# One attention kernel: values as streamed probabilities or as column-tile weights

## What is computed

```python
x = x + attention(layernorm(x))        # 32 query heads, 8 key/value heads, head size 32, rotary, causal
x = x + fake_quant(layernorm(x)) @ fake_quant(ctx)
x = x + fixed_point_linear(layernorm(x))   # Q8.8 integers, 16 bit results
# attention, per batch and head:
scores = q @ k.T / sqrt(32); scores[causal] = min
ctx = softmax(scores) @ v              # heads h*4 .. h*4+3 share one k and v
```

## Time and profile before

| what | value |
|---|---|
| median of three runs | 586.71 us |
| profiled execution | 589.05 us, span of its instructions 587.2 us |
| TensorE matmul busy | 492.4 us (84%) |
| VectorE, ScalarE, GpSimd busy | 394.1, 327.5, 259.5 us |
| mean granted TensorE clock | 0.952 |
| attention groups | from 146.65 us to about 434.4 us of the span |

### The profile page before, as it was taken

The page is one execution under the profiler, slowest core; times in us unless marked ns, Lnnn a source line. Parts: engine busy times, 40 slices in busy tenths (PEclk is TensorE's granted clock), DMA queues, the critical chain, the costliest instruction groups (busy, mean ns, idle before and its releaser), DMA issues.

```text
span 587.2 us, 12002 instructions
## 1 busy us (share of the span) xinstructions
PE 492.4 (84%) x4050; PEld 279.8 (48%) x4050; DVE 394.1 (67%) x763; ACT 327.5 (56%) x395; POOL 259.5 (44%) x242
## 2 busy tenths in 40 slices
PE   2678998587689889898899999999798999976776
PEld 2356643233355555455565555555443444444333
DVE  5875277464587788787866877887439466767436
ACT  2654233200577766677757888888943531456533
POOL 5030113324367779767784555456652734230000
PEclk9898998779999999999969999999999899987899
DMA  9821366522301110011103222112355110000015
GB/s 313 255 86 59 115 178 173 148 88 89 90 2 47 45 45 18 29 44 45 48 22 133 91 93 90 39 52 91 109 204 220 42 36 19 1 2 1 33 42 215
DMA packets 42616, 50.68 MB, mean 86 GB/s; under 512 B 4049, under 2 KB 32337, under 8 KB 42577
## 3 DMA queue, kind: packets, MB, share of 16 engines
q1 hardware_dynamic: 25792, 41.69, 21.3%
q10 hardware_dynamic: 16784, 8.46, 5.0%
HBM read 40.57 MB, written 9.44 MB: 85 GB/s over the span
## 4 chain that ended last, share of the span: by engine, by line
PE 37%; DVE 19%; DMA 12%; issue 11%; POOL 10%; ACT 7%; SPq 3%; DVEq 0%; ACTq 0%; POOLq 0%
PE ps L1352 10%; DMA rope_scratch<-s1reg 7%; PE ps L1457 4%; PE ps L1220 4%; DVE stat L725 4%; PE ps L1179 3%; PE ps L1414 3%; DMA qstack<-rope_scratch 3%; POOL s1reg L1092 3%; PE ps L1240 2%; PE ps L1207 2%; DVE mt L781 2%; PE ps L1255 2%; POOL wkv L1100 2%; POOL s1reg L1111 2%
## 5 line engine op out<-in xcount | busy, mean ns | idle before, releaser
L781 DVE TENSOR_REDUCE mt<-ps 128x1 f32<-128x512 f32 (+3 forms) x256 | 113.2, 484 | 50.3 <-PE ps L1222 47.9
L1179 PE MATMUL ps<-xT,wqx 128*128 128x512 f16 x384 | 99.3, 397 | 3.9 <-DVE s1reg L772 3.5
L1352 PE MATMUL ps<-wo_reg,xT 128*128 128x512 f16 x384 | 94.2, 384 | 2.3 <-DVE wqx L813 2.2
L1111 POOL TENSOR_TENSOR s1reg<-s1reg 128x1280 f16<-128x1280 f32 x32 | 83.7, 2614 | 28.1 <-ACT s1reg L510 26.5
L503 ACT ACTIVATE s1reg<-ps 128x1280 f32<-128x1280 f32 x64 | 78.9, 1233 | 24.4 <-PE ps L1242 22.5
L1220 PE MATMUL ps<-kreg,qstack 96*128 (+4 forms) x256 | 72.4, 314 | 22.1 <-DVE mt L781 15.3
L510 ACT ACTIVATE s1reg<-s1reg 128x1280 f16<-128x1280 f32 x64 | 81.3, 1270 | 2.8
L1240 PE MATMUL ps<-qstack,kreg 98*128 (+4 forms) x256 | 58.0, 303 | 11.8 <-DMA qstack<-mrow 8.3
L797 DVE TENSOR_TENSOR s1reg<-s1reg 128x1280 f16<-128x1280 f32 x32 | 53.3, 1667 | 15.1 <-ACT s1reg L510 15.1
L1100 POOL TENSOR_TENSOR wkv<-wkv 128x128 f32<-128x128 f32 x64 | 35.1, 549 | 62.4 <-DVE rcp L803 62.3
L1179 PEld LDWEIGHTS ps<-xT,wqx 128*128 128x128 f16 (+1 forms) x384 | 35.6, 102 | 43.7 <-issue 13.8
(11 more groups left out here) (123 smaller groups left out, 790.0 us busy)
## 6 DMA issues: line engine op xcount, KB each, us to landing
s1reg<-in_ctx SPq DMA_DIRECT2D x16, 512.0 KB, 4.6
qstack<-rope_scratch SPq DMA_DIRECT2D x48, 128.0 KB, 2.4
rope_scratch<-s1reg SPq DMA_DIRECT2D x40, 128.0 KB
qstack<-in_x SPq DMA_DIRECT2D x8, 512.0 KB, 5.3
s1reg<-in_L_attn_Wq ACTq DMA_DIRECT2D x8, 512.0 KB, 4.8
s1reg<-in_L_attn_Wo ACTq DMA_DIRECT2D x8, 512.0 KB, 5.3
s1reg<-in_x SPq DMA_DIRECT2D x16, 256.0 KB, 2.9
out<-s1reg SPq DMA_DIRECT2D x7, 512.0 KB, 2.7
```

The source lines that it names most:

```text
L781: nc.vector.reduce_max(mt[:, 2 * hp + e, qt:qt + 1], ps[:, 3 + e, 0:P * (qt + 1)], AX.X).then_inc(s_max, 1)
L1111: nc.gpsimd.tensor_tensor(pl[:, j % 2, :], ebuf[:, j % 2, :], ph[:, j % 2, :], ALU.subtract).then_inc(pl_done[1], 1)
L1179: last = mm(out_ap, w(ws, k), xT[:, xs, KT * b + k, :], start=(k == 0 and n == 0), stop=(k == KT - 1 and n == 2))
L1352: last = mm(ps[:, bank, :], xT[:, os, KT * b + k, t], wo_sb[:, ws, 4 * h:4 * h + 4, k, :], start=(k == 0 and n == 0), stop=(k == KT - 1 an ...
```

## The change

The probabilities become the streamed operand and the values the weights. `values(G)` is one block for four heads. It has five products: for the denominators a 128x32 block of ones as weights, with the high and then the low parts of the probabilities streamed; for the numerators the high values with the high probabilities, the low values with the high, and the high values with the low. Each product has four key blocks k with 512, 384, 256 and 128 columns and for each the four heads, head j writing output partitions 32j to 32j+31: 80 products and 80 weight loads per group. The result is already transposed, in bank NUM (5) and, for the sums, bank DEN (6). `out_transpose`, `pv_out`, `inverse_sum` and `head_out` go. VectorE's `heads_norm` takes the reciprocal of the whole DEN bank (128x512) and multiplies it with NUM into `osum`; it stands where `ot_low` stood, before maxima 6 and 7. `ot_high` reads `osum`, moves behind `p_high(G,2)` on ScalarE, and `ot_low` moves to GpSimd. In phase D `p_low(G,2)` moves from VectorE to GpSimd. Probabilities get six buffers instead of two, so that `p_high` and `p_low` no longer wait for the values of two heads before. `values(G-1)` stands in group G behind `scores_t(G,1)`. All loops are written out as 16 groups.

```diff
-VW = 2 * DH + 1
+VW = 2 * DH
+SLOTS = 6
...
-        def attention_c(eng, body):
-            body(0, 0, False, True)
-            with eng.Fori(1, KV - 1) as g:
-                body(g, g, True, True)
-            body(KV - 1, KV - 1, True, True)
-
-        def attention_d(eng, body):
-            body(KV, 0, True, True, 0, 0)
-            body(KV + 1, 1, True, True, 0, 1)
-            with eng.Fori(1, KV // 2 - 1) as p:
-                for u in range(2):
-                    body(p * 2 + (KV + u), p * 2 + u, True, True, p, u)
-            body(NG - 2, KV - 2, True, True, KV // 2 - 1, 0)
-            body(NG - 1, KV - 1, True, False, KV // 2 - 1, 1)
+        def attention_c(body):
+            for g in range(KV):
+                body(g, g, g > 0, True)
+
+        def attention_d(body):
+            for g in range(KV):
+                body(KV + g, g, True, g < KV - 1, g // 2, g % 2)
...
             def exp(G, j):
                 act.wait_ge(st_done, G * 4 + (j + 1))
-                if not (isinstance(G, int) and G == 0 and j < 2):
-                    act.wait_ge(*pl_count(G, j))
+                if G or j >= 2:
+                    act.wait_ge(pl_done[(j + 2) % HG], G + (j >= 2))
...
             def p_high(G, j):
                 act.wait_ge(e_done, G * 4 + (j + 1))
-                if not (isinstance(G, int) and G == 0 and j < 2):
-                    act.wait_ge(pv_done, G * 4 + (j - 1))
-                nc.scalar.activation(ph[:, j % 2, :], ebuf[:, j % 2, :], ACT.Copy).then_inc(ph_done, 1)
+                p_free(act, HG * G + j)
+                nc.scalar.activation(ph(HG * G + j), ebuf[:, j % 2, :], ACT.Copy).then_inc(ph_done, 1)
...
             def ot_high(G):
-                act.wait_ge(ot_done, G + 1)
-                nc.scalar.activation(xT[:, 0, one(G), :], ps[:, OT:OT + 1, :], ACT.Copy).then_inc(ot_hi, 1)
+                act.wait_ge(o_norm, G + 1)
+                nc.scalar.activation(xT[:, 0, G, :], osum, ACT.Copy).then_inc(ot_hi, 1)
...
                 p_high(G, 1)
-                pv_out(G, 0)
+                exp(G, 2)
+                p_high(G, 2)
                 if tail:
                     ot_high(G - 1)
-                exp(G, 2)
-                p_high(G, 2)
                 if ahead:
                     max_row(G + 1)
-                pv_out(G, 1)
...
+            def heads_norm(G):
+                dve.wait_ge(den_done, G + 1)
+                nc.vector.reciprocal(rsum[:, :], ps[:, DEN, :]).then_inc(o_rcp, 1)
+                dve.wait_ge(pv_done, G + 1)
+                dve.wait_ge(o_rcp, G + 1)
+                if G:
+                    dve.wait_ge(ot_lo, G)
+                nc.vector.tensor_tensor(osum, ps[:, NUM, :], rsum[:, :], ALU.mult).then_inc(o_norm, 1)
...
                 ahead_max(5)
                 middle()
                 if tail:
-                    ot_low(G - 1)
+                    heads_norm(G - 1)
                 ahead_max(6, 7)
                 if ahead:
                     split_max(G + 1)
-                p_low(G, 2)
-                inverse_sum(G, 1)
+                if G < KV:
+                    p_low(G, 2)
...
+            def ot_low(G):
+                pool.wait_ge(ot_hi, G + 1)
+                nc.gpsimd.tensor_tensor(xT[:, 1, G, :], osum, xT[:, 0, G, :], ALU.subtract).then_inc(ot_lo, 1)
 
             def body(G, g, tail, ahead, p=None, u=None):
+                p_low(G, 1)
+                if p is not None:
+                    p_low(G, 2)
                 if tail:
-                    head_out(G - 1, 3)
-                p_low(G, 1)
-                head_out(G, 0)
-                head_out(G, 1)
+                    ot_low(G - 1)
                 p_low(G, 3)
-                head_out(G, 2)
...
-            def values(G, j):
-
-                low, before = pl_count(G, j)
-                pe.wait_ge(low, before + 1)
-                if not (isinstance(G, int) and G == 0 and j == 0):
-                    pe.wait_ge(pvs_done, G * 4 + j)
-                for qt in range(TT):
-                    for k in range(qt + 1):
-                        at = SEG[k] + P * (qt - k)
-                        for n, part in enumerate((ph, pl)):
-                            last = mm(ps[:, PV, VW * qt:VW * qt + VW], part[:, j % 2, at:at + P],
-                                      vext[:, k, one(G), :], start=(k == 0 and n == 0), stop=(k == qt and n == 1))
-                last.then_inc(pv_done, 1)
...
+            def values(G):
+
+                for j in range(HG):
+                    pe.wait_ge(pl_done[j], G + 1)
+                pe.wait_ge(mrow_ready, min(G + 2, NG))
+                if G:
+                    pe.wait_ge(o_norm, G)
+
+                def product(bank, part, weight, first, final):
+                    for k in range(TT):
+                        n = T - P * k
+                        for j in range(HG):
+                            last = mm(ps[DH * j:DH * j + DH, bank, P * k:T], weight(k), part(HG * G + j)[:, SEG[k]:SEG[k] + n],
+                                      start=(first and k == 0), stop=(final and k == TT - 1))
+                    return last
+
+                product(DEN, ph, lambda k: ones_h[:, 0:DH], True, False)
+                product(DEN, pl, lambda k: ones_h[:, 0:DH], False, True).then_inc(den_done, 1)
+                product(NUM, ph, lambda k: vext[:, k, G, 0:DH], True, False)
+                product(NUM, ph, lambda k: vext[:, k, G, DH:2 * DH], False, False)
+                product(NUM, pl, lambda k: vext[:, k, G, 0:DH], False, True).then_inc(pv_done, 1)
...
                 ahead_scores(1)
+                scores_t(G, slot, 1)
                 if tail:
-                    values(G - 1, 3)
-                scores_t(G, slot, 1)
+                    values(G - 1)
                 ahead_scores(2)
...
-                    pe.wait_ge(pvs_done, 4 * NG)
+                    pe.wait_ge(o_norm, NG)
```

More of the change, by code:

```diff
@@ L123, in build, with ph, pl @@
         wkvf = wkv[:, :, :, :, :].rearrange("p s n k c -> p (s n k c)").bitcast(F32)
-        ogrp = wkvf[:, 0:512].rearrange("p (t c) -> p t c", t=TT)
-        osum = wkvf[:, 512:640].rearrange("p (t c) -> p t c", t=TT)
-        pvs = wkvf[:, 640:640 + 2 * TT * VW].rearrange("p (s t c) -> p s t c", s=2, t=TT)
+        osum = wkvf[:, 3072:3584]
+        p_slots = [(s1reg, 2560), (s1reg, 3840), (wkvf, 0), (wkvf, 1792)]
+        ppair = [region[:, at:at + SCORES].bitcast(F16).rearrange("p (s n) -> p s n", s=2) for region, at in p_slots]
+        ppair += [more[:, 2 * SCORES * i:2 * SCORES * i + 2 * SCORES].rearrange("p (s n) -> p s n", s=2) for i in range(2)]
+        def ph(head):
+            return ppair[head % SLOTS][:, 0, :]
+        def pl(head):
+            return ppair[head % SLOTS][:, 1, :]
         ctx_st = s1reg[:, 5120:7168].rearrange("p (s n) -> p s n", s=2)
@@ L1227, in max_transpose @@
                     pe.wait_ge(rope_mul, 12)
-                if not (isinstance(G, int) and G < 2):
-                    pe.wait_ge(ot_lo, G - 1)
+                if G >= 2:
+                    pe.wait_ge(o_rcp, G - 1)
                 nc.tensor.transpose(mt_ps(G), mh[:, :, :].rearrange("p s n -> p (s n)"), ident_h).then_inc(mt_done, 1)
```

116 lines of the change are left out of this document (32 added, 84 removed).

## The result

The changed kernel takes 680.9 us (median of four runs, 678.88 to 681.2) against 586.13 us for the kernel before beside it (583.99 to 589.8): ratio 1.157, 95% interval 1.152 to 1.161. The profiled execution takes 680.65 us with a span of 678.9 us; before it was 589.05 and 587.2. So 91.6 us are to be explained on the profiled executions, where the prediction had 57 or 58. The mean granted TensorE clock is 0.888, before 0.952. TensorE's matmuls are busy 526.3 us (78% of the span), VectorE 437.9, ScalarE 309.4, GpSimd 233.0.

The account below looks back on a forecast made before the run. Bound: nearly full TensorE and a loop through VectorE's maxima. Phase C +18, group 8 +2, phase D +25, last group +4, group 0 -1, loops -3, clock +12: +57 or 58, 589.05 to 647 us (645 against the median); range 611 to 685.

Parts of the forecast that it names:

- The loop through VectorE: Every group: what stands in VectorE's list before maxima 6 and 7 delays the next group; 3.2 us more there.
- The reciprocal: VectorE's 128x512 division in heads_norm: 3.2 us, bounds 0.68 and 4.3.
- slow division: Rival: VectorE's reciprocal takes eight plain passes, 4.3 us, making the kernel 661 us; chance 0.2.
- The values block: TensorE's 80 products per group: four column tiles stream together, taking 3.1 us.
- The layout of a group: Phase D laid out from durations: max_transpose at 17.6 us, next start 21.1, 4.2 more than 16.92; phase C 20.8.
- The clock: TensorE's pause from 12.9 to 17.6 lowers its clock in each group: 0.8 us each, 12 in all, between 0 and 1.7.
- Group 8: Given phase C's period of 20.8 us, against 18.95 before: 2 us more.
- Last group: No scores ahead; values end at 21.9, column_sums at 24.3 us instead of 20.0: 4.3 more.
- Loops: Looped groups cost 0.37 us more than unrolled, 3.7 for ten; 3 us taken off.
- Cheap division: Rival: VectorE's reciprocal runs as any operation there, 0.68 us, giving 600 us; chance 0.07.
- Tiles in turn: Rival: TensorE's column tiles do not overlap, values take 11.0 us per group, about 760 us in all; chance 0.08.
- a kernel bound by TensorE: Rival: VectorE's stretch between maxima 5 and 6 stays under 0.7 us, groups take 16.0, kernel 559 us; chance 0.03.

Follow-up runs that it names:

- short_division: Changed kernel with the reciprocal run on only 4 of the 512 columns of the denominator bank: 600.12 us, ratio 1.016.
- scalar_division: Changed kernel with narrower low-part waits in groups 8 and 9 and the reciprocal on ScalarE as exp(-ln x): 591.98 us, ratio 1.0065.
- norm_late_pieces: Changed kernel, heads_norm behind split_max except last group, values in four pieces, narrower waits in groups 8 and 9, p_low(G,2) and ctx on GpSimd: 648.2 us.
- kept_warm: Changed kernel plus 15 zero-weight products of 512 columns per group where TensorE would wait for VectorE: 655.7 us, ratio 1.110.
- group8_wait: Changed kernel, each slice of group 8's output projection waiting for its own low part only, not all eight: 676.12 us, ratio 1.147.
- before_unrolled: The kernel before with its two hardware loops written out, nothing else: 585.09 us, ratio 0.992.
- low_part_behind: Changed kernel with GpSimd's ot_low(G-1) behind its last p_low, except in group 8: 670.27 us, ratio 1.135.

## Why the prediction was right, and where its terms were off

**The loop through VectorE** (right). The prediction read from the earlier trace rows that everything ahead of maxima 6 and 7 is on the path of every group. short_division and scalar_division take the division off VectorE in two ways and give back 80.8 and 84 us; TensorE's wait of 3.35 us lies where it was said to lie, and in group 9 the division starts 12.21 us after the group's start, for 12.2.

**The reciprocal** (right). 3.35 us against 3.2, from ten short ones with a slope of 12 ns for two elements. The Trainium skill (VectorE: DVE Perf Modes, First, the fixed hardware budget), read as eight cycles per element, gave an estimate of 4.3; the trace has 3.35, 6.2 ns per element beside the fixed part of 0.17, so the case that the prediction called slow division did not come.

**The values block** (right). 2.83 us against 3.1, tiles together. The Trainium skill (TensorEngine Tiling (Array Packing), Key Properties) has a drain at a change of tiling mode; this trace has at most 0.15 us from the last pair of the block to the next product (366.54 to 366.69), so no drain of a size that counts.

**The layout of a group** (right but for one instruction). From first product to `max_transpose` 17.6 were forecast and 18.69 measured (359.37 to 378.06). 0.8 in this group, 0.56 on average over the run, is `split_max` behind GpSimd; 0.15 is the division's own excess over 3.2, and the last 0.15 lies at the joints. The step that failed is in the queue order and in the layout: the prediction asked of `ot_low` in its new list on GpSimd who waits for it, and not what it would meet there, and gave `split_max` 0.4 us as if it ran alone. The Trainium skill (SBUF — State Buffer, Who interferes with whom) has VectorE and GpSimd share one pair of ports under an exclusive lock, in the faster modes of `tensor_scalar` and with two inputs in SBUF; the trace agrees, 0.98 for 0.17 us with both ends within 0.03 us, and so do the pairs of norm_late_pieces. That ports are the cause stands in the Trainium skill alone; the runs show the meeting and its price.

**The clock** (mechanism right, size wrong). The prediction had a low stretch after a pause in every group, and took 0.8 us of an interval from 0 to 1.7; no row stands behind the 1.7. The low stretch came in every group, and its price lies above the whole interval: the distance from `max_transpose` to the next start is 5.2 to 5.5 us in all but one of groups 1 to 14 (4.59 in group 7) where the prediction had 3.5, 1.85 more in group 9. Where kept_warm keeps the clock, it gives back 2.4 us per group in phase C and 2.1 in D, more than 1.85 because the distance is then 3.2 and not 3.5. That is some 29 us in 13 groups where 10 were taken. The reason given for half, that the DMA behind `max_transpose` would hide some, was too weak by the prediction's own numbers: its 2.7 us of TensorE work are 5.4 at half the clock, which is 1.9 over the 3.5, and the trace has it so. TensorE is busy in all 3.40 us of the stretch from 378.10, and its last fillers run from 381.02 to the next start. Before, one such stretch followed a pause of 1.73 us and lasted to about 305 us (0.50 from 296.5 to 304), longer than the one piece in the earlier trace rows; no row spoke for the lower half.

**Group 8** (missed). The prediction gave it the price of phase C. It is where the output projection of batch 0 begins, and that waits for the last `ot_low` of batch 0, now on GpSimd behind two low parts (the division is not what holds it: the wait is 6.19 us in short_division too). The question "who waits for the moved step" had been answered for the usual group alone. It came 7.4 us over the forecast: 3.0 are this wait (group8_wait), 1.9 are what every group is over, and 2.5 stay open. The trace shows where to look for them, not why: the clock is at 0.50 for the first eight microseconds of this group (330 to 338), and its values block takes 4.2 us in place of 2.83.

**Last group** (nearly right). 26.4 against 24.3. GpSimd and ScalarE were where the forecast had them within 0.8 us (the last low part ends at 522.6, 19.6 after the start, for 18.8). The block takes 4.4 us there (its last product starts at 527.3) in place of 3.1, most of it at the low clock after 5.04 us of waiting:

```profile
522.96 0.45 PE L1224 MATMUL ps<-s1reg,ones_h 128*32 128x512 f16 x2 [5.04 <-POOL wkv L1075]
...
523.81 0.67 PE L1224 MATMUL ps<-s1reg,ones_h 128*32 128x512 f16 x2
...
526.81 0.40 PE L1224 MATMUL ps<-s1reg,vext 128*32 128x512 f16 x2
```

**Loops** (right): 3 forecast, 4.7 measured by before_unrolled, for the kernel before.

**The sum.** Per group of phases C and D the forecast with its clock was 21.6 and 21.9 and the trace has 23.5 and 23.9. The missing 1.9 and 2.0 are the stretch behind `max_transpose` (0.9 to 1.2 beyond 3.5 + 0.8), `split_max` (0.5 to 0.8), and 0.2 to 0.4 for the division's excess and the joints. Over 13 groups that is 25 of the 34 us by which the sum fell short; group 8 is 7.4 more, the last group about 1.6. The loops' 3 us and group 0's 1 are not to be seen as terms of their own, which is 4 the other way, and the head and tail of the program, 4.2 us shorter, cancel them. That the time lies in the range is partly luck: the range had slow division (16 us) and slow tiles (10) in it, which did not come, and the clock beyond its upper end, `split_max` and group 8 took their room.

**Rivals.** Cheap division was priced at 600, and short_division is nearly that case: 600.12. The match is luck: its price stood for periods of 18.3 and 18.6 and as much for group 8; measured are 17.6, 17.9 and 26.9, and the 9 us saved in thirteen groups are the 9 lost in one. Tiles in turn (760) and a kernel bound by TensorE (559) are refuted, the second because with the division gone phase D still takes 17.9 and not 16.0. Why it does, when the columns streamed by values on TensorE take about as long as before (2.83 for 2.5 us), is open: pieces and a later place of the block did nothing, and the explanation that VectorE's list then waits one row further on is argued from one timeline and not shown.

## What to carry to other kernels

Before an operation is moved to a unit where it looks small, work out its length in the new shape and ask which product of TensorE is released by what stands behind it; a pause made there is paid twice when the clock falls after it. Of a moved operation ask three things: who waits for it in the usual round, who waits for it in the one round that differs, and what runs beside it in its new place. The cheapest place for a long operation is the queue in which nobody waits, even if it takes longer there (3.8 us on ScalarE against 3.35 on VectorE, and 84 us less).

## What the runs showed of the hardware that was not expected

- Column tiles overlap whatever the order in the list: head by head or block by block, 80 products take 2.87 and 2.83 us, and tiles whose first products stand eight places apart start within 0.03 us.
- An operation on VectorE and one on GpSimd that meet are done one behind the other: 0.98 for 0.17 us, 3.76 for 1.5, 3.29 for 1.48, and on GpSimd 2.41 for 1.15. The maxima, which read PSUM, showed nothing of the kind: four of 512 columns take 2.52 us beside GpSimd's `ctx` operation in norm_late_pieces and beside its low part in low_part_behind, for 2.63 in the earlier trace rows.
- Fifteen useless products of 3.4 us in the pause of each of 14 groups made the kernel 25 us faster.
- ScalarE's Ln and Exp each bring a table load of 1.28 us, 32 of them in a run; none shows in the periods, which are no longer than those of short_division.
